# One gathered row in four added by VectorE instead of an identity product, in a two-layer graph network on one core

## The reference

```python
for l in range(n_layers):                       # 2 layers
    m = jnp.concatenate([h[row], h[col]], axis=-1)      # row = src, col = dst
    m = jax.nn.relu(m @ msg_W1[l].T + msg_b1[l])
    m = m @ msg_W2[l].T + msg_b2[l]
    agg = jax.ops.segment_sum(m, col, num_segments=h.shape[0])
    upd = jnp.concatenate([h, agg], axis=-1) @ upd_W[l].T + upd_b[l]
    h = _layer_norm(h + upd, ln_g[l], ln_b[l])
```

## Time and profile before

| | us |
|---|---|
| three runs of the kernel, median | 3485.89 (3481.67 to 3485.97) |
| the profiled execution, its own time | 3484.03 |
| its span in the profile | 3482.3 |
| first layer's edge stage, first gather to last `combine` | 1572.23 to 2107.20 |
| second layer's edge stage, first gather to last `combine` | 2527.16 to 3062.7 |
| TensorE busy, share of the span | 87% |
| VectorE busy, share of the span | 78% |

### The profile page before, as it was taken

How to read it: one execution, slowest core, us unless ns; L and a number is a source line. 1 busy time by engine, 2 the same in 40 slices (tenths; PEclk the granted TensorE clock), 3 DMA queues, 4 the chain that set the end, 5 groups by cost and what they waited for, 6 DMA issues and landing times. The chain is left out here.

```text
span 3482.3 us, 93313 instructions
## 1 busy us (share of the span) xinstructions
PE 3018.6 (87%) x25704; PEld 2717.8 (78%) x25704; DVE 2703.6 (78%) x8634; ACT 2378.6 (68%) x5642; POOL 1852.4 (53%) x1782
## 2 busy tenths in 40 slices
PE   4976656777767789998999998999989999989998
PEld 3753334555533389888999998999989999989998
DVE  9999968888856688886777775666667777778888
ACT  3779936777733278886777774666667777758888
POOL 0000046667755433337776775555377777755553
PEclk9989988999979999999999999999999999999999
DMA  0027736777659999997776645999977666468886
GB/s 21 2 74 227 225 95 173 221 218 218 194 159 348 315 320 363 357 351 227 224 218 204 189 133 191 328 327 328 312 226 223 216 205 186 130 190 261 261 262 214
DMA packets 460711, 777.80 MB, mean 223 GB/s; under 512 B 113688, under 2 KB 115864, under 8 KB 460392
## 3 DMA queue, kind: packets, MB, share of 16 engines
q1 hardware_dynamic: 355046, 548.85, 48.1%
q10 hardware_dynamic: 67714, 147.73, 12.4%
q0 software_dynamic: 37632, 77.15, 9.0%
HBM read 451.50 MB, written 321.78 MB: 222 GB/s over the span
## 5 line engine op out<-in xcount | busy, mean ns | idle before, releaser
L883 DVE SCALAR_TENSOR_TENSOR edges_acc<-edges_acc,keep,edges_ps_a 128x128 f32 (+1 forms) x2352 | 820.3, 349 | 272.7 <-issue 143.8
L851 POOL DMA_INDIRECT ring<-table_p,esrc x784 | 794.4, 1013 | 304.6 <-issue 204.9
L1011 PE MATMUL edges_ps_m<-ring,ident 128*128 x3136 | 609.6, 276 | 32.8 <-POOLq L840 32.8
L1012 PE MATMUL edges_ps_m<-edges_q_ring,edges_turned 128*128 x3136 | 608.6, 276 | 0.0
L1011 PEld LDWEIGHTS edges_ps_m<-ring,ident 128*128 128x128 f32 x3136 | 478.6, 193 | 33.4 <-issue 33.2
L1012 PEld LDWEIGHTS edges_ps_m<-edges_q_ring,edges_turned 128*128 128x128 f32 x3136 | 478.5, 193 | 0.0
L979 ACT ACTIVATE edges_msg<-edges_ps_m 128x512 f32<-128x512 f32 x392 | 234.2, 598 | 295.0 <-PE edges_ps_m L1012 288.7
L1021 PE MATMUL edges_ps_a<-edges_onehot,edges_msg 128*128 128x128 f32 x3136 | 414.0, 275 | 0.0
L851 POOL DMA_INDIRECT ring<-table_h,esrc x344 | 328.4, 955 | 136.9 <-issue 96.9
L1021 PEld LDWEIGHTS edges_ps_a<-edges_onehot,edges_msg 128*128 128x128 f32 x3136 | 381.7, 192 | 0.0
L868 DVE TENSOR_TENSOR edges_onehot<-iota,drel 128x512 f32<-128x512 f16 x441 | 304.8, 692 | 95.4 <-PE edges_ps_a L1021 94.6
(11 more groups left out here) (315 smaller groups left out, 6902.1 us busy)
## 6 DMA issues: line engine op xcount, KB each, us to landing
table_z<-nodes_z_t SPq DMA_DIRECT2D x196, 256.0 KB, 4.9
table_p<-nodes_p_out SPq DMA_DIRECT2D x196, 256.0 KB
table_q<-nodes_q_out ACTq DMA_DIRECT2D x196, 256.0 KB
edges_q_ring<-table_q SPq DMA_DIRECT2D x196, 256.0 KB, 5.0
edges_d_ring<-table_d ACTq DMA_DIRECT2D x98, 512.0 KB
table_t<-edges_acc SPq DMA_DIRECT2D x196, 256.0 KB
nodes_in_a<-table_t SPq DMA_DIRECT2D x196, 256.0 KB
nodes_in_z<-table_z SPq DMA_DIRECT2D x196, 256.0 KB, 4.3
```

The source lines that it names most:

```text
L851: nc.gpsimd.indirect_dma_start(out=ring[:, e % RE * W:e % RE * W + P], out_offset=None, in_=table[:, :], in_offset=bass.IndirectOffsetOnAx ...
L883: nc.vector.scalar_tensor_tensor(out=to, in0=to, scalar=m.keep[:, s:s + 1], in1=ps_a[:, i % AR, where(j):where(j) + F], op0=ALU.mult, op1= ...
L1011: nc.tensor.matmul(to, m.ident[:], rows[j], start=True, stop=False)
L1012: last = nc.tensor.matmul(to, turned[:, i % QR, j * P:(j + 1) * P], slots[j], start=False, stop=True)
```

## The change

In the edge stages of the two layers, `combine` leaves out the identity product of the first step of each batch: three identity products and four products with Q remain. The gathered row tile of that step is added to `ps_m` by VectorE instead, in a new function `add_row`, once TensorE has finished the batch. VectorE does it at the head of its turn, as `add_row(i-1)`, `hot(i)`, `chain(i-3)`. The address of the tile comes from `steps`, of which VectorE now loads four words every second batch. ScalarE's relu waits for the addition and no longer for TensorE. GpSimd counts freed tile slots by the additions. `QR` goes from three to four.

```diff
-HR, QR, BEHIND = 3, 3, 2
+HR, QR, BEHIND = 3, 4, 2
...
-                        pool.wait_ge(s_seg if degrees else s_pq, third(ends, k))
+                        pool.wait_ge(s_seg if degrees else s_added, third(ends, k))
...
+                def add_row(i):
+                    if i % 2 == 0:
+                        word[0] = load(mybir.EngineType.DVE, m.steps[0:1, 2 * i:2 * i + 4])
+                    row = ring[:, bass.ds(word[0][i % 2 * 2] // (1 << 7) % RE * W, P)]
+                    nc.vector.lower_ap(row)
+                    dve.wait_ge(s_pq, i + 1)
+                    nc.vector.tensor_tensor(ps_m[:, i % QR, 0:P], ps_m[:, i % QR, 0:P], row, ALU.add).then_inc(s_added, 1)
...
                 for i in range(NB + (lag + 2 if degrees else lag)):
+                    if not degrees and 1 <= i < NB + 1:
+                        add_row(i - 1)
...
-                        act.wait_ge(s_pq, i + 1)
+                        act.wait_ge(s_added, i + 1)
...
                     for j in range(4):
                         to = ps_m[:, i % QR, j * P:(j + 1) * P]
-                        nc.tensor.matmul(to, m.ident[:], rows[j], start=True, stop=False)
-                        last = nc.tensor.matmul(to, turned[:, i % QR, j * P:(j + 1) * P], slots[j], start=False, stop=True)
+                        if j > 0:
+                            nc.tensor.matmul(to, m.ident[:], rows[j - 1], start=True, stop=False)
+                        last = nc.tensor.matmul(to, turned[:, i % QR, j * P:(j + 1) * P], slots[j], start=j == 0, stop=True)
```

More of the change, by code:

```diff
@@ L781, in edge_stage @@
             d_ring = sb("d_ring", [P, DR, DB * CH], F16)
-            ps_m = pb("ps_m", 512, QR)
+            ps_m, s_added = pb("ps_m", 512, QR), sem("s_added")
         else:
@@ L862, in _ @@
                 dve.wait_ge(s_zero, 1)
-                slots = {}
+                slots, word = {}, {}
                 def hot(i):
@@ L1004, in combine @@
                     landed = due(i)
-                    rows, slots = addressed([row(i, j) for j in range(4)]), addressed([slot(i, j) for j in range(4)])
+                    rows, slots = addressed([row(i, j) for j in range(1, 4)]), addressed([slot(i, j) for j in range(4)])
                     pe.wait_ge(s_turned, 2 * i + 2)
```

## The result

The changed kernel takes 3515.43 us (median of 4 runs, 3512.03 to 3519.08), the kernel before 3485.18 beside it (4 runs, 3481.67 to 3485.97). The ratio is 1.0086, with a 95% interval of 1.0074 to 1.0098: slower by 30 us, which is more than the 0.2% that a measurement can tell. The profiled execution took 3516.94, with a span of 3515.2.

A forecast was written before the change was run, and what follows sets the result against it. TensorE bounds the kernel at 2.68 us a batch; afterwards VectorE needs 2.36 + 0.19 + 0.08 + 0.03 + 0.02 = 2.68. So 392 x (2.68 - 2.68) + 1 on the profiled 3484.0, 2 below the median: 3487, range 3455 to 3530.

The forecast's parts named there:

- TensorE needs 2.45 us after: TensorE in the edge stages: one product in twelve removed, 0.223 us a batch, leaving 2.45 us.
- A batch without a load, 2.36: VectorE's queue: 1.15 us chain issue, 0.27 until the addition starts, 0.94 for four addresses; 2.36 us in all.
- Loads, 0.21 and 0.11: VectorE's loads a batch: `steps` 0.19 plus 0.02 us for stretched ones, `slots` 0.08 plus 0.03.
- Nothing else in the queue: VectorE's batch: beyond the load-free batch and the loads, pauses of its queue were counted as 0.
- The loop has 1 us to spare: Addition, relu, segment, combine: below 4.4 us until the next addition may run, wanted after 5.36; QR = 4 gives nothing.
- TensorE's gap, waiting for `msg`: TensorE was to show some 0.2 us of gap a batch ahead of line 1032.
- GpSimd covers freeing tiles later: GpSimd's gathers: tiles freed about 1 us later, covered by 7.8 us to spare before TensorE's last batch.
- the second: VectorE's addition is dearer in PSUM, 0.35 us instead of 0.28: 2.75 us a batch, 3514; chance 0.14.
- Rival 1: VectorE's `steps` loads cost more than four words' worth, 0.60 us: 2.79 us a batch, 3530; chance 0.18.
- The sibling of rival 2: VectorE's addition blocks GpSimd's gathers as the one-hot seems to: +40 us, 3525; chance 0.04.
- Rival 3: VectorE's stalls are rarer than counted, loads at their medians: 2.63 us a batch, 3467; chance 0.16.
- Rival 4: VectorE's loads and addresses are hidden, TensorE stays the bound at 2.45 us; GpSimd's gathers cap it at 3452; chance 0.12.

The follow-up runs named there:

- experiment 6: Changed kernel without the addition and without an identity product in its place; 3441.69 us, ratio 0.9870 (first try, on a slow chip: 3976.41 us).
- Experiments 3 and 4: 3: changed kernel loading four words of `steps` every batch, 3595.74 us; 4: changed kernel with one 16-word load in eight batches, no `slots` load, 3450.24 us.
- experiments 1 and 2: 1: kernel before with only QR = 4, 3488.46 us; 2: changed kernel with QR = 3, 3517.25 us.
- experiment 7: Changed kernel with one 16-word load in eight batches, TensorE keeping its identity product in each fourth batch; 3475.74 us, ratio 0.9974.
- experiment 5: Changed kernel adding the identity table at a fixed address, without the `steps` load; 4059.81 us on a slow chip, 3432.30 us when repeated on another.

## Why the prediction was right and where it was off

The time lies in the range (3455 to 3530), 28 us above the forecast, and in the main the forecast's mechanism is what happened. Its reading as "no change" was wrong: a real loss of 0.9% came out. The step at fault is the total of VectorE's batch, "2.68 us a batch, what TensorE needs today"; it measured 2.755.

- **TensorE needs 2.45 us after.** Right; shown without a gap in experiment 6.
- **VectorE sets the pace.** Right: no wait for TensorE in the stretch, relu released by VectorE, batches alternating between 2.4 and 2.8.
- **A batch without a load, 2.36.** It is 2.41, which is 0.05 too little and about two thirds of the miss. The step "From the addition's start the four addresses take their 0.94" was off: the chain comes 1.00 us after the addition's start at the median (1799.91 to 1800.91; 0.98 in the next batch). The first address operation starts 0.05 us after the addition, where it started 0.01 after the one-hot in the kernel before, and the operations take some 0.02 longer together. The other two terms held: 1.15, and 0.26 for 0.27. That it was "By datapath" 2.36 too was a coincidence: the datapath stands free for 0.12 us ahead of the chain (1800.79 to 1800.91).
- **Loads, 0.21 and 0.11.** Right to 0.005, the median and the stretched ones. Experiments 3 and 4 show that they are paid in full.
- **Nothing else in the queue.** Wrong by 0.015 to 0.019, the rest of the table with its pauses. The kernel before has them too, hidden by its wait; the forecast carried over only those of the loads.
- **The loop has 1 us to spare, QR gives nothing.** Right that it has time to spare, by experiments 1 and 2; how much, no run shows.
- **TensorE's gap, waiting for `msg`.** Not as forecast: of its 24 us only 1.1 stand ahead of line 1032, and 22.7 ahead of line 1023, the first product of `combine`, 0.13 us a batch. What holds it there was not tested.
- **GpSimd covers freeing tiles later.** Its waits for the releasing engine grew from 19.4 to 29.9 us, but its gathers got shorter, 973 ns for 1010, and TensorE waited little for it (5.0 us). It cost nothing that can be seen.

Of the rivals, the second named the time (3514), and not for its reason: it has the addition at 0.35 us, and the addition takes 0.299; and in a batch without a load the addresses' start counts, not the addition's length. Rival 1 asked for loads above 0.42 at the mean; they have 0.39 and 0.38. The rule of the Trainium skill ("DMA: Bandwidth & Descriptors", Latency and other measured facts), a floor of about 600 ns, is not what this chip shows for four words: 0.347 at the median of 98. The sibling of rival 2, that the addition lengthens gathers, fell: they got shorter. It also rested on a misreading, that every second gather takes 1.13; in the whole first layer 107 of 392 take over 1.05. Rival 3 (stalls rarer) fell. Rival 4's cap is real: with VectorE relieved the layer stops at 3432 to 3442 us, 10 to 20 us under the 3452 that I gave, and not at TensorE's 3398.

The miss is 0.07 us in 2.68. A forecast that sets one engine's new sum equal to another's old one to the last digit has no "no change" as its likeliest case: it has a slope on both sides, and what had been left out (pauses, later starts) lay on one of them.

## What to carry to other kernels

When work moves to an engine that had been waiting, price its instruction queue, not its datapath: all that the wait had hidden (loads of words, addresses, pauses of the queue) is paid from then on, so group the loads first, which here turned a loss of 0.9% into a gain of 1%. Hand work back only in a turn in which the engine that gives it up is late; elsewhere the saving becomes a wait that holds the queue. Even there it saves less than its own length where queue work had run underneath it (0.18 us for 0.31). And look for the next bound before expecting more: here it was GpSimd's 392 gathers, 490 us a layer at the least.

## What the runs showed of the hardware

- Loading words from SBUF into registers on VectorE goes by the words: 0.347 us for 4, 0.597 for 8, 1.099 for 16 at the median, which is 0.063 us a word and 0.1 beside it. Single loads stretch to 1.1 for 4 words and 1.5 for 16.
- A gather is long when it begins while VectorE's one-hot runs. The shortest take 0.94 us. In the first layer 107 of 392 took over 1.05 us in the kernel before, 42 in the changed one and 1 in experiment 7. All of these, and all gathers of over 1.05 us in the layers of every kernel traced here, began while a one-hot was running. In the first layers, on the chips of normal speed, each ended 0.81 to 0.82 us after that one-hot did. None of those that began at another time took over 0.99 us, those that began during an addition included. That is how the traces order them in time; no run moved the one-hot by itself.
- One of the chips ran the kernel before in 3999 us and not in 3486, with a granted clock of 0.92 in the profiled run of experiment 5 against 0.97 elsewhere.
